# One change of three parts in a fused attention and feed-forward kernel: a residual's normalised rows and first convolution taps on another engine, a bias as matrix products, and up-products ahead of the second batch's fusion

## What the reference computes

```python
residual = x                                  # here x is layernorm(x) of the outer x
h = _rmsnorm(x, norm_w)
h = _linear(h, in_w, in_b)
gate, val = h[..., :DI], h[..., DI:]          # DI = 512
gate = sigmoid(gate)
a = _dwconv(val, dwa_k, dwa_b, 1, 2)          # 4 taps
a = (a @ A) @ Bm
b = _dwconv(val, sym_k, sym_b, 4, 4)          # 9 taps
b = _linear(silu(b), pw_w, pw_b)
a = _linear(a, ha_w, ha_b)
b = _linear(b, hb_w, hb_b)
y = gate * _linear(concat([a, b]), fuse_w, fuse_b)
return residual + _linear(y, out_w, out_b)    # added to the outer x
...
h = layernorm(x); h = gelu(bitlinear(h, w1, b1)); h = bitlinear(layernorm(h), w2, b2)   # block 3
```

## Time and profile before

| | |
|---|---|
| median of 3 runs | 912.66 us (911.25 to 912.73) |
| the profiled execution, whole | 912.04 us |
| its span | 910.2 us |
| TensorE busy (matmul) | 874.1 us, 96% |
| VectorE, ScalarE, GpSimd busy | 609.7, 474.4, 136.2 us |

### The profile page before, as it was taken

One profiled execution on the slowest core, in us unless ns is written; L12 is line 12 of the kernel. 1 busy time (PEld: TensorE's weight loads), 2 busy tenths in 40 slices (PEclk: granted clock), 3 DMA queues, 4 the chain that ended last, 5 costly groups with the idle time before them and its releaser, 6 DMA issues.

```text
span 910.2 us, 15328 instructions
## 1 busy us (share of the span) xinstructions
PE 874.1 (96%) x6037; PEld 519.5 (57%) x6037; DVE 609.7 (67%) x1068; ACT 474.4 (52%) x958; POOL 136.2 (15%) x141
## 2 busy tenths in 40 slices
PE   7799999999999999999999999999999999999998
PEld 3355544444556665555554578755784784656745
DVE  5879677777886556888883389886724327469352
ACT  4242566777776556777778962314411310668221
POOL 5434011111000000000000071010100005336100
PEclk9899999999999999999999999999999999999999
DMA  9978934546433311333533260084643805000000
GB/s 354 276 202 193 209 110 124 147 125 159 115 71 71 81 36 36 70 71 71 137 123 132 94 249 2 1 277 140 231 185 134 329 1 186 1 1 1 1 1 24
DMA packets 55081, 108.49 MB, mean 119 GB/s; under 512 B 5408, under 2 KB 38176, under 8 KB 49824
## 3 DMA queue, kind: packets, MB, share of 16 engines
q1 hardware_dynamic: 51568, 97.26, 37.6%
q10 hardware_dynamic: 3440, 10.22, 3.7%
HBM read 93.58 MB, written 13.89 MB: 118 GB/s over the span
## 4 chain that ended last, share of the span: by engine, by line
PE 82%; DVE 10%; ACT 3%; issue 2%; DMA 2%; POOL 0%; ACTq 0%; SPq 0%; DVEq 0%
PE psum L2019 14%; PE psum L2001 13%; PE psum L1967 12%; PE psum L2421 6%; PE psum L2449 6%; PE psum L1944 6%; PE psum L2553 5%; PE psum L1934 4%; PE psum L2186 3%; DVE arena L1501 3%; PE psum L2618 2%; DVE arena L1252 2%; PE psum L2603 2%; PE psum L2173 2%; PE psum L2642 1%
## 5 line engine op out<-in xcount | busy, mean ns | idle before, releaser
L1252 DVE TENSOR_REDUCE arena<-psum 128x1 f32<-128x1024 f32 x256 | 301.1, 1219 | 102.4 <-PE psum L1967 101.9
L823 ACT ACTIVATE arena<-psum 128x512 f32<-128x512 f32 x512 | 263.6, 604 | 67.8 <-PE psum L2001 66.5
L1967 PE MATMUL psum<-arena 96*128 96x512 bf16 x512 | 153.2, 381 | 10.0 <-DMA arena<-qparts 4.8
L2001 PE MATMUL psum<-arena 99*128 99x256 bf16 x1024 | 155.1, 274 | 3.9 <-ACT arena L814 1.7
L2019 PE MATMUL psum<-arena 128*32 128x256 f32 x2048 | 137.0, 385 | 0.0
L2001 PEld LDWEIGHTS psum<-arena 99*128 99x128 bf16 x1024 | 80.6, 97 | 98.6 <-ACT arena L823 36.7
L2019 PEld LDWEIGHTS psum<-arena 128*32 128x32 f32 x2048 | 53.4, 109 | 74.2 <-ACT arena L823 30.7
L1934 PE MATMUL psum<-arena 128*128 128x512 f32 x128 | 61.7, 609 | 6.0 <-DMA arena<-ctxT 5.5
L682 POOL TENSOR_TENSOR arena<-arena 128x512 bf16<-128x512 f32 x34 | 41.3, 1214 | 174.5 <-DVE arena L1238 171.8
L1967 PEld LDWEIGHTS psum<-arena 96*128 96x128 bf16 x512 | 48.9, 98 | 29.1 <-DVE arena L1252 11.4
L1944 PE MATMUL psum<-arena 128*128 128x256 f32 x256 | 63.8, 386 | 0.0
(11 more groups left out here) (269 smaller groups left out, 1014.1 us busy)
## 6 DMA issues: line engine op xcount, KB each, us to landing
kparts<-arena SPq DMA_DIRECT2D x32, 384.0 KB, 3.0
arena<-kparts SPq DMA_DIRECT2D x32, 384.0 KB, 5.2
arena<-kparts SPq DMA_DIRECT2D x32, 256.0 KB, 5.7
arena<-mask SPq DMA_DIRECT2D x8, 1024.0 KB, 5.2
arena<-ctx SPq DMA_DIRECT2D x2, 4096.0 KB, 17.5
arena<-ctxT SPq DMA_DIRECT2D x14, 512.0 KB, 6.0
arena<-ctxT ACTq DMA_DIRECT2D x10, 512.0 KB, 15.4
arena<-mask ACTq DMA_DIRECT2D x4, 1024.0 KB, 9.9
```

The lines of the kernel that those rows point to most:

```text
L823: nc.scalar.activation(PR[step % 4][:, pair * CH:(pair + 1) * CH], exp_bank(step, pair), ACT.Exp)\
L1252: nc.vector.tensor_reduce(MX[g % 2][:, col:col + 1], unit_banks(n).rearrange("p b n -> p (b n)"), AX.X, ALU.max).then_inc(s_maxed, 1)
L1967: last = nc.tensor.matmul(out, q, KST[g % 2][0:ROWS, quarter, j, half * CH:(half + 1) * CH], start=True, stop=not masked, skip_group_check ...
L2001: last = nc.tensor.matmul(heads[:, u, :], KST[gg % 2][0:KROWS, kc // 8, j, kc % 8 * P:(kc % 8 + 1) * P], QST[0:KROWS, b, G * g + j, :], st ...
```

## The change

1. **x plus its norm.** GpSimd's twelve instructions go. VectorE computes `GROWN = 1 + 1/sd` for the four tiles and `NEGM = -mean/sd` for each (five small instructions ahead of the taps), and ScalarE does `X = X * GROWN + NEGM`, one instruction for each tile.
2. **out_b.** `project_out` begins each tile with a product of one row of ones and the bias row, and accumulates the four others on it. It waits for the gates one by one, and no longer for all four ahead of the first product.
3. **First taps.** Six of the eight first taps (all but those of batch 0, pair 0) move from VectorE to ScalarE, two behind `copy_in(0, ..)` and four behind `sigmoids(0, 0)`.
4. **Gates of batch 0** stand between the taps of the last pair, one after taps 2, 4, 6 and 8 each.
5. **TensorE's order.** `convolve_a(1)` and `project_ha(1)`, which stood before the fusion and before `project_out(0)`, now stand behind the first quantised tile's transpose and behind its up-products, and all of `fuse(1, m)` behind them. ScalarE's `copy_a(1)` and `copy_ha(1)` move along, behind the quantised tile's copy and ahead of the first gelus. The Gelu table is loaded ahead of `copy_hb(1)`. The banks of two up-products are exchanged.

```diff
-            pool.wait_ge(ln_step, 2 * TT + 2)
-            for i in range(TT):
-                nc.gpsimd.tensor_scalar(HL[:, i, :], X[:, i, :], MV[:, 2 * i:2 * i + 1], SD[:, 4 + i:5 + i],
-                                        ALU.subtract, ALU.mult).then_inc(x_summed, 1)
...
-                nc.gpsimd.tensor_tensor(HL[:, i, :], HL[:, i, :], row("out_b"), ALU.add).then_inc(x_summed, 1)
...
-                nc.gpsimd.tensor_tensor(X[:, i, :], X[:, i, :], HL[:, i, :], ALU.add).then_inc(x_summed, 1)
...
+            def first_tap(b, m):
+                signal(nc.scalar.activation(CB[:, m, batch(b)], VAL[:, m, b, 4 - LEFT_B:4 - LEFT_B + S], ACT.Identity,
+                                            scale=col("sym_k", TAPS_B * m), bias=col("sym_b", m)), "c_in_copied")
+
+            act.wait_ge(on["c_in_copied"], in_step(0, 3))
+            first_tap(0, 2)
+            first_tap(0, 3)
             copy_in(1, 0, 4)
             sigmoids(0, 0)
+            act.wait_ge(on["c_in_copied"], in_step(1, 3))
+            for m in range(IT):
+                first_tap(1, m)
             copy_in(1, 4, 8)
+            act.wait_ge(ln_step, 2 * TT + 7)
+            for i in range(TT):
+                nc.scalar.activation(X[:, i, :], X[:, i, :], ACT.Identity, scale=GROWN[:, i:i + 1],
+                                     bias=NEGM[:, i:i + 1]).then_inc(x_summed, 1)
             copy_hbpw(0)
...
             copy_hb(0)
             copy_ha(0)
             sigmoids(1, 0)
-            copy_a(1)
             sigmoids(1, 1)
-            copy_ha(1)
+            nc.scalar.activation(TABLES[:, 0:1], ONES[:, 0:1], ACT.Gelu)
             copy_hb(1)
-            nc.scalar.activation(TABLES[:, 0:1], ONES[:, 0:1], ACT.Gelu)
...
             copy_quantised_tile(0)
+            copy_a(1)
+            copy_ha(1)
             gelus(0, 2)
...
+            dve.wait_ge(ln_step, 2 * TT + 2)
+            nc.vector.tensor_scalar(GROWN, SD[:, 4:8], 1.0, None, ALU.add).then_inc(ln_step, 1)
+            for i in range(TT):
+                nc.vector.scalar_tensor_tensor(out=NEGM[:, i:i + 1], in0=mean[:, i:i + 1, 0], scalar=-1.0,
+                                               in1=SD[:, 4 + i:5 + i], op0=ALU.mult, op1=ALU.mult).then_inc(ln_step, 1)
...
+            gates_at = {2: 0, 4: 1, 6: 2, 8: 3}
...
-                            if k == 0:
-                                dve.wait_ge(on["c_in_copied"], 8 * b + m + 1)
+                            if k == 0 and (b or pair):
+                                dve.wait_ge(on["c_in_copied"], first_tap_step(b, m))
+                            elif k == 0:
...
-            for m in range(IT):
-                gate(0, m)
+                        if b and pair and k in gates_at:
+                            gate(0, gates_at[k])
...
-                pe.wait_ge(on["c_gated"], IT * (b + 1))
                 for i in (2 * b, 2 * b + 1):
-                    linear_rows(psum[:, OUT_BANKS[i], 0:256], tok(YG, i), WOUT, False, "c_out")
+                    rows = tok(YG, i)
+                    if b:
+                        pe.wait_ge(on["c_gated"], IT * b + 1)
+                    bias_rows([psum[:, OUT_BANKS[i], 0:256]], row("out_b")[0:1, :])
+                    for k in range(IT):
+                        if i == 2 * b:
+                            pe.wait_ge(on["c_gated"], IT * b + k + 1)
+                        last = nc.tensor.matmul(psum[:, OUT_BANKS[i], 0:256], rows[k], WOUT[:, k, :],
+                                                start=False, stop=(k == IT - 1), skip_group_check=True)
+                    last.then_inc(on["c_out"], 1)
...
                 project_ha(0)
-                convolve_a(1)
                 pe.wait_ge(on["c_ha_copied"], 2)
                 pe.wait_ge(on["c_hb_copied"], 2)
                 for m in range(IT):
                     fuse(0, m)
-                project_ha(1)
                 project_out(0)
                 pe.wait_ge(on["c_gated"], IT)
                 project_hb(1)
-                pe.wait_ge(on["c_ha_copied"], 4)
+                pe.wait_ge(on["x_ready"], TT + 2)
                 pe.wait_ge(on["c_hb_copied"], 4)
                 turn_quantised(0, 0)
-                fuse(1, 0)
-                pe.wait_ge(on["x_ready"], TT + 2)
+                convolve_a(1)
                 pe.wait_ge(on["d_turned_copied"], 1)
                 pe.wait_ge(on["w_quantised"], 6)
                 project_up(0, 0)
                 project_up(0, 1)
+                project_ha(1)
+                pe.wait_ge(on["c_ha_copied"], 4)
+                fuse(1, 0)
                 fuse(1, 1)
```

More of the change, by code:

```diff
@@ L269, in build, with in_step, first_tap_step @@
         QHT = [b16(at, 1024).rearrange("p (k n) -> p k n", k=FT) for at in (40832, 41344, 4352, 4864)]
+        def in_step(b, j):
+            return 10 * b + j + 1 + (4 if b and j >= 4 else 0)
+        def first_tap_step(b, m):
+            return 7 + m if b == 0 else 15 + m
         IN_BANKS = ((4, 7), (1, 2))
@@ L273, in build @@
         QUANT_BANK = (1, 3)
-        UP_BANKS = ((7, 0, 2, 1), (7, 3, 7, 3))
+        UP_BANKS = ((7, 2, 0, 1), (7, 3, 7, 3))
         DOWN_BANKS = (5, 6, 3, 7)
@@ L381, in build @@
         NEGM = f32(at, 4); at += 4
+        GROWN = f32(at, 4); at += 4
         NHALF = f32(at, 4); at += 4
@@ L715, in _ @@
                                             ALU.mult).then_inc(on["c_a_weights"], 1)
-            pool.wait_ge(ln_step, 2 * TT + 2)
-            for i in range(TT):
-                nc.gpsimd.tensor_scalar(HL[:, i, :], X[:, i, :], MV[:, 2 * i:2 * i + 1], SD[:, 4 + i:5 + i],
-                                        ALU.subtract, ALU.mult).then_inc(x_summed, 1)
-            for i in range(TT):
-                pool.wait_ge(x_summed, i + 1)
-                nc.gpsimd.tensor_tensor(HL[:, i, :], HL[:, i, :], row("out_b"), ALU.add).then_inc(x_summed, 1)
-            for i in range(TT):
-                pool.wait_ge(x_summed, TT + i + 1)
-                nc.gpsimd.tensor_tensor(X[:, i, :], X[:, i, :], HL[:, i, :], ALU.add).then_inc(x_summed, 1)
             powers = [3 + 1]
@@ L936, in sigmoids @@
                 for m in (2 * pair, 2 * pair + 1):
-                    act.wait_ge(on["c_conv_b"], 2 * TAPS_B * (2 * b + pair) + 2 * (TAPS_B - 1) + m % 2 + 1)
+                    act.wait_ge(on["c_conv_b"], (2 * TAPS_B - 2) * (2 * b + pair) + 2 * (TAPS_B - 1) + m % 2 + 1)
                     signal(nc.scalar.activation(SB[:, m, batch(b)], CB[:, m, batch(b)], ACT.Sigmoid), "c_sigmoid")
@@ L1485, in add_mixed, with taps_by @@
                 ask_root(first, last, 1.0 + 1e-5, 1e-5 * 1e-5)
+            def taps_by(b, pair, k, m):
+                return (2 * TAPS_B - 2) * (2 * b + pair) + 2 * k + m % 2 + 1
+            gates_at = {2: 0, 4: 1, 6: 2, 8: 3}
             for b in range(B):
@@ L1498, in _ @@
                             else:
-                                dve.wait_ge(on["c_conv_b"], 2 * TAPS_B * (2 * b + pair) + 2 * (k - 1) + m % 2 + 1)
+                                if k > 1 or not (b or pair):
+                                    dve.wait_ge(on["c_conv_b"], taps_by(b, pair, k - 1, m))
                                 nc.vector.scalar_tensor_tensor(out=out, in0=src, scalar=tap, in1=out,
@@ L1600, in copy_cq @@
                   .then_inc(on["e_cq_copied"], 1)
-            dve.wait_ge(x_summed, 3 * TT)
+            dve.wait_ge(x_summed, TT)
             add_mixed(0, 1, TT)
@@ L2342, in mix @@
                     project_in(1, j)
-                pe.wait_ge(on["c_in_copied"], 12)
+                pe.wait_ge(on["c_in_copied"], in_step(1, 3))
                 for m in range(IT):
@@ L2357, in mix @@
                 convolve_a(0)
-                pe.wait_ge(on["c_in_copied"], 16)
+                pe.wait_ge(on["c_in_copied"], in_step(1, 7))
                 pe.wait_ge(on["c_hbpw_copied"], IT + 2)
```

1 line of the change is left out of this document (added).

## The result

| | before | after |
|---|---|---|
| median of 6 runs each | 912.84 us (911.25 to 913.73) | 919.68 us (918.64 to 920.29) |
| profiled execution, its span | 912.04, 910.2 us | 919.69, 917.9 us |

The ratio is 1.0072, with a 95% interval of 1.0062 to 1.0082: slower by 6.8 us, where 914.5 (+1.8) was predicted with 916.8 as the upper end. The direction was the one forecast as likeliest; the size was not.

What follows compares the result with a forecast made beforehand. The prediction took TensorE, not VectorE, to set `fuse(0)`; added work and waits ended `project_out(1)` 1.66 us later and the hidden tile's transpose 1.80 later, so 912.66 + 1.8 = 914.5 us, range 911.6 to 916.8.

Steps and rivals of the forecast that it cites:

- VectorE's idle time ahead of the silu: Last pair on VectorE: silu waits for ScalarE's sigmoids, so 4 us of the 6 us gained are idle.
- the pairs: Pairs of channel groups on VectorE: 7.0 us each without first taps and without GpSimd's additions beside them.
- The up-products: TensorE's up-products: to start at 579.15 instead of 580.50, 1.4 us earlier.
- The three waits on TensorE: Waits for batch 0's copies 0.64, the first quantised tile 0.92, and `project_ha(1)`'s copies ahead of `fuse(1, 0)` 0.70 us.
- The wait for the last gate: TensorE's 1.25 us wait for batch 1's last gate goes, since bias row and three products stand before it.
- The chain from `gate(1, 1)` to the quantised tile: VectorE's work up to the quantised hidden tile: 10.46 us as before, putting `turn_hidden(0)` at 595.96, +1.80.
- VectorE's relief: VectorE in the mixing block: 6 us lighter, most of it running into a wait because TensorE sets `fuse(0)`.
- The rival "faster": VectorE's relief brings `fuse(0)` earlier; `project_out(1)` ends 3.8 us earlier, 908.9 us; chance 0.13.
- Bias rows ... I take 0.2225: Four one-row products in `project_out`: eight records at 0.2225 us, the pace of their neighbours, 1.78 us on TensorE.
- The upper bound, 0.38 a record: Bias rows at 381 ns a record, as a product that doesn't overlap its neighbours: 3.05 us.
- All that follows to 605.43 hangs on this transpose: +1.8 us.: From `turn_hidden(0)` to the key scores everything moves along with the transpose, +1.8 us.
- slower by more: Dearer bias rows (+1.3), or new waits half a microsecond longer at two or three places: +3.1, 915.8 us; chance 0.17.

Runs made afterwards that it cites:

- e1: Changed kernel with four more keep-awake products in the branch that never runs: 915.39 us, ratio 1.0030.
- e5: Changed kernel without bias products (VectorE adds the bias), twenty never-run products in the other branch: 914.84 us, ratio 1.0024.
- e4: Changed kernel without bias products (VectorE adds the bias to X), sixteen never-run products keeping the count near 192: 916.12 us, ratio 1.0034.
- e2: Kernel before with sixteen more keep-awake products in the branch that never runs: 916.63 us, ratio 1.0043.
- e3: Changed kernel with the bias product over all 128 rows (identity times bias) in place of one row of ones: 917.68 us, ratio 1.0056.
- e9: Changed kernel with 128 never-run products (256 instructions), returning the count to 192: 919.56 us, ratio 1.0066.
- e8: Kernel before with twenty never-run products in the branch not taken: 913.07 us, ratio 0.9999.
- e7: Changed kernel with bias on VectorE, but TensorE's and ScalarE's order of the kernel before, padded past the boundary: 912.53 us, ratio 0.9995.
- e10: Filled-waits version with the first hidden tile finished, turned and projected ahead of the second tile's parts and `project_out(1)`: 909.81 us, ratio 0.9962.
- e6: Changed kernel, bias on VectorE, padded, with `convolve_a(1)` ahead of the quantised tile's transpose and `project_ha(1)` right behind it: 912.86 us, ratio 1.0000.

## Why the prediction was wrong

**Right.** `fuse(0)` was to start at 561.12, the trace has 562.24 - 1.13 = 561.11. VectorE's idle time ahead of the silu was to be 4 us and is 3.92; the pairs take 7.0; the gates of batch 0 cost nothing, since TensorE reaches the last gate's product behind the bias row. The up-products were to start at 579.15 and do at 580.89 - 1.13 = 579.76, later by about what the two bias rows of batch 0 cost beyond the forecast. The three waits on TensorE were to be 0.64, 0.92 and 0.70. The rows show 0.56, 0.86 and 0.56 of idle time, counted from modelled ends; by the prediction's own measure, from start to start at the pace of the products, they are 0.64, 578.82 - 574.35 - 3.56 = 0.91 and 583.36 - 581.77 - 0.89 = 0.70. The wait for the last gate is gone. The chain from `gate(1, 1)` to the quantised tile was to last 10.46 us, as before, and takes 597.57 - 587.12 = 10.45. VectorE's relief runs into TensorE's own time: against the padded kernel before it is worth 0.43 us. The rival "faster" had a start of `project_out(0)` at 564.8 as its sign (its own sum used 562.8, a slip between the two), and it came at 569.34 - 1.13 = 568.21, where 568.2 was forecast.

**Mis-sized: "Bias rows ... I take 0.2225".** The mechanism held, the term did not: 0.63 us for a row instead of 0.445, and 0.14 more for the eight records behind it, 4 x 0.77 = 3.1 us worked out, 2.88 by removal, instead of 1.78. The upper bound, 0.38 a record, gave 3.05; it was the right end of the range, and the nearest row in columns and type was the wrong one to go by. At the key scores the rows cost 1.35 in all once the gap is away (e1 against e5), since VectorE is the last without them.

**Failed: "All that follows to 605.43 hangs on this transpose: +1.8 us."** `turn_hidden(0)` did start about there, at 598.22 - 1.13 = 597.09, 1.1 us behind the forecast because of the bias rows. What followed did not keep its distance: 605.43 - 594.16 = 11.27 us before, 613.06 - 598.22 = 14.84 after. The gap is 2.69 of these 3.57, and the rest fits the pace of the products at the low clock. Without the gap (e1) the key scores come at 73.92, so it is worth 77.91 - 73.92 = 4.0 us of 6.5, and the time, 915.39, would have been inside the predicted range. I had counted what the change adds to the time of the path, and not that it makes the code ahead of the branch's end 32 TensorE instructions longer, nor looked at what stands where the branch ends. The stretch from the transpose to 605.43 was taken as fixed, a term of nothing without a reason. No rival had it; "slower by more" had only more of the costs that were already in the sum.

The parts, at the key scores: the place of the code 4.0, the bias rows 1.35, the order 1.8, VectorE's relief and the hidden gap -0.64; together 6.5. They depend on the order in which they are taken away. With the bias rows taken first (e4) they are worth 77.91 - 73.40 = 4.5, with the clock that then stayed high, and the gap 0.83; the sum of the two is the same 5.3. The prediction's chain without its two bias rows ahead of `gate(1, 1)` (0.89) is +0.9 at the transposes; e5, which has none, shows 61.21 - 60.14 = +1.07. With the bias rows e1 shows 63.08 - 60.14 = +2.94 there, where +1.80 was forecast. So the path was followed rightly up to this transpose, with one term too small.

**Open.** What TensorE waits for at the boundary, and why work goes on 2.7 to 2.9 us after the first behind the jump, no run shows. That the low clock behind the gap follows from the idle time is argued from their order in the trace: it fell to 0.50 behind the gaps of the changed kernel, e2, e3 and e9 (2.69, 2.63, 2.45 and 2.46 us) and stayed at 1.00 behind the 2.32 us of e4, and no run shows what made the difference. The split of the 4.0 us into 2.8 of gap and 1.2 of clock rests on e4 and on one execution each. The mask loads, which wait for the transposes, are later by the gap too; they show no wait on TensorE up to the key scores, but what they cost behind them was not tried.

## What to carry to other kernels

Behind the end of this kernel's branch a few more instructions, even ones that never run, moved the boundary to or from a place where TensorE had little work ahead of it: at the key scores it was worth 4.0 us in the changed kernel, 3.3 in the kernel before (e2 against e8) and 0.8 where another engine was late anyway (e4 against e5). So when a change leaves a gap that waits for "issue", pad the branch that isn't taken by a handful of instructions before judging the change, and, going by the 2.7 to 2.9 us seen here, have some 3 us of work between the end of a branch and the next boundary. The bias as a product of one row wasn't cheaper here than one of 128 rows but dearer (0.63 us against 0.44, e3), and the 6 us or so that VectorE was relieved of were worth 0.43 at the key scores, with TensorE full beside it (e7 against e8); what paid was to ask which tile the next stage needs first (key scores 71.38 - 66.74 = 4.64 us earlier, e10 against e6).

## What the hardware showed that was not expected

- The position of code, counted modulo 256 instructions: the changed kernel at 919.68 us (count 192), 915.39 (200, e1) and 919.56 (192 again, 256 instructions on, e9), and the kernel before at 913.07 (200, e8) and 916.63 (192, e2).
- An idle gap of 2.69 us was followed by a granted clock of 0.65, 0.50, 0.50 and 0.65 in four windows of a microsecond, some 1.2 us lost by the comparison with e4. In e1, without the gap, each window from 600 to 604 has 1.00, and in e4, with a gap of 2.32 us, each from 598 to 604 too.
- A one-row f32 product of 256 columns took 0.63 us to the next, one of 128 rows 0.44 (e3); the load of the one row's stationary operand wasn't overlapped with the product ahead (0.33 us idle before it).
